# The tail of an attention and quantized feed-forward kernel: last scores and exponentials by tile, small scales moved to GpSimd, decodes moved to ScalarE

## What is computed

```
q     = x + embed[stage][:, None]          # one bias per row
prob  = softmax(q @ f.T)                   # 256x256
a     = prob @ f
xh    = a @ H                              # Hadamard 256x256, scaled
scale = max(max|xh| over the row, 1e-5) / 7
xq    = clip(round(xh / scale), -8, 7) * scale
wq    = ternary(weight) * mean|weight row|
out   = x + xq @ wq.T
```

## Time and profile before

| | |
|---|---|
| median of 3 runs | 108.36 us (107.94 to 108.78) |
| the profiled execution | 108.61 us, span 106.8 us |
| TensorE busy | 97.4 us (91% of the span), 799 products |
| VectorE busy | 87.7 us (82%) |
| ScalarE busy | 76.1 us (71%) |
| GpSimd busy | 47.1 us (44%) |
| DMA | 14.71 MB, mean 138 GB/s |

### The profile page before, as it was taken

How to read it: one execution, slowest core, us unless ns; L and a number is a source line. 1 busy time by engine, 2 the same in 40 slices (tenths; PEclk the granted TensorE clock), 3 DMA queues, 4 the chain that set the end, 5 groups by cost and what they waited for, 6 DMA issues and landing times.

```text
span 106.8 us, 2584 instructions
## 1 busy us (share of the span) xinstructions
PE 97.4 (91%) x799; PEld 90.9 (85%) x799; DVE 87.7 (82%) x216; ACT 76.1 (71%) x200; POOL 47.1 (44%) x66
## 2 busy tenths in 40 slices
PE   5969899999999999999999999999999998995640
PEld 2439799899999999999999999999999998995410
DVE  1085699798989898989989898989898989699880
ACT  3255986969696978787878787878788865780610
POOL 5034699404343435343435353535353534058050
PEclk9999999999999999999999999999999999999855
DMA  3984632425253664947282728282722222202214
GB/s 68 256 298 120 257 112 30 169 53 199 49 173 134 175 215 119 228 111 237 96 227 86 245 68 262 54 289 49 292 51 98 49 98 49 98 0 98 98 53 143
DMA packets 14850, 14.71 MB, mean 138 GB/s; under 512 B 8054, under 2 KB 8956, under 8 KB 14844
## 3 DMA queue, kind: packets, MB, share of 16 engines
q1 hardware_dynamic: 14688, 14.62, 45.1%
q10 hardware_dynamic: 156, 0.01, 0.1%
HBM read 8.73 MB, written 4.19 MB: 121 GB/s over the span
## 4 chain that ended last, share of the span: by engine, by line
PE 72%; DVE 14%; ACT 4%; DMA 3%; issue 3%; ACTq 1%; DVEq 0%
PE score_bank L461 19%; PE xh_bank L461 18%; PE fh_bank L461 12%; PE prob_bank L450 6%; PE out_bank L516 5%; PE f_bank L450 5%; PE q_bank L450 5%; DMA stage_of<-itok_dram 3%; ACT prob L672 2%; DVE prob_lo L841 1%; DVE least_scale L863 1%; DVE fh_lo L841 1%; DVE raw_scale L819 1%; DVE xh_bank L996 1%; DVE result L1002 1%
## 5 line engine op out<-in xcount | busy, mean ns | idle before, releaser
L359 POOL TENSOR_TENSOR result<-scaled,x_all 128x512 f32<-128x512 f32 x13 | 16.7, 1281 | 24.3 <-DVE scaled L827 24.3
L351 POOL TENSOR_TENSOR code<-code,magic 128x512 bf16<-128x512 f32 x13 | 13.5, 1040 | 14.8 <-ACT code L650 14.8
L650 ACT ACTIVATE code<-xh_bank,inv_scale 128x256 f32<-128x256 f32 x30 | 12.8, 486 | 4.8 <-DVE inv_scale L953 2.8
L672 ACT ACTIVATE prob<-score_bank,neg_max 128x256 f32<-128x256 f32 x32 | 15.0, 478 | 0.9 <-DVE neg_max L868 0.9
L841 DVE TENSOR_TENSOR prob_lo<-prob_bank,prob_hi 128x512 fp32r<-128x512 f32 x16 | 11.1, 691 | 5.2 <-ACT prob_hi L662 5.2
L666 ACT CAST fh_hi<-fh_bank 128x512 fp32r<-128x512 f32 x16 | 9.4, 589 | 7.9 <-PE fh_bank L461 7.7
L461 PE MATMUL score_bank<-f_hi,q_hi 128*128 128x256 f32 x64 | 14.1, 302 | 0.3 <-ACT prob L672 0.3
L461 PE MATMUL fh_bank<-had,f_hi 128*128 128x256 f32 x64 | 14.0, 299 | 0.0
L641 ACT CAST f_hi<-f_bank 128x512 fp32r<-128x512 f32 x15 | 8.8, 587 | 5.7 <-PE f_bank L450 5.7
L461 PE MATMUL score_bank<-f_lo,q_hi 128*128 128x256 f32 x64 | 12.8, 282 | 0.0
L461 PE MATMUL score_bank<-f_hi,q_lo 128*128 128x256 f32 x64 | 12.8, 282 | 0.0
(11 more groups left out here) (129 smaller groups left out, 232.5 us busy)
## 6 DMA issues: line engine op xcount, KB each, us to landing
f_nat<-f_dram SPq DMA_DIRECT2D x16, 256.0 KB, 2.8
x_all<-x_dram SPq DMA_DIRECT2D x16, 256.0 KB, 3.0
out_dram<-result SPq DMA_DIRECT2D x14, 256.0 KB, 2.0
out_dram<-result SPq DMA_DIRECT2D x4, 128.0 KB, 1.8
w_raw<-weight_dram SPq DMA_DIRECT2D x1, 256.0 KB, 4.8
code_t<-code SPq DMA_TRANSPOSE x13, 2.5
had_block<-hadamard_dram SPq DMA_DIRECT2D x1, 64.0 KB, 3.9
embed_sb<-embed_dram ACTq DMA_DIRECT2D x1, 6.0 KB
```

Source lines behind the costliest of these rows:

```text
L351: nc.gpsimd.tensor_tensor(as_rows(code16[:, b.k]), as_rows(code), magic[:, :].broadcast_to([P, W]), ALU.subtract).then_inc(code16_ready, 1)
L359: nc.gpsimd.tensor_tensor(result[:, b.k], as_rows(scaled[:, b.k]), x_all[:, b.at], ALU.add).then_inc(result_ready, 1)
L650: return nc.scalar.activation(to[:, t], xh[:, t], ACT.Copy, bias=MAGIC, scale=inv_scale[:, b.k, t:t + 1])
L672: a = nc.scalar.activation(prob[:, t], score_bank[:, t], ACT.Exp, bias=neg_max[:, b.k, t:t + 1], accum_out=row_sum[:, b.k, t:t + 1])
```

## The change

After the loop, five things change. TensorE turns batch 14's probabilities ahead of the last scores; the last scores go into f_bank and q_bank, a tile each with a signal of its own, and VectorE's maximum and ScalarE's exponential follow by tile. On TensorE, mix of 14 stands ahead of 13's ternary products, and the Hadamard products of 15 ahead of the code turn of 13. The two least_scale multiplies and the output scales of 14 and 15 are made on GpSimd; VectorE keeps the reciprocals of the sums, and takes those of batch 14's scales in one instruction. Both decodes of 128x512 are on ScalarE. The last batch's result has its own buffer, last_result, so the wait for batch 13's store is gone. In GpSimd's list a final step (batch 12's result) is drawn behind the two least_scale multiplies.

```diff
@@ tiles and banks
+        last_result = sb("last_result", [P, W], F32)
+        last_score_banks = [f_bank, q_bank]
@@ SyncE, last stores
-                sp.dma_start(out_dram[last.at, :, cols], result[:, last.k, cols]
+                sp.dma_start(out_dram[last.at, :, cols], last_result[:, cols]
@@ GpSimd, after the loop
-            for i in range(B - 2, B + LAG_OUT - 3):
+            for i in range(B - 2, B):
                 step(peeled(i), dma_turns=i - LAG_QUANT < turned_by_dma)
+            for b in (second_last, last):
+                pool.wait_ge(prob_ready, b.at + 1)
+                pool.wait_ge(raw_scale_ready, b.at - 1)
+                nc.gpsimd.tensor_scalar(least_scale[:, b.k], row_sum[:, b.k], MIN_ABS / POS, None,
+                                        ALU.mult).then_inc(least_ready, 1)
+            step(peeled(B), dma_turns=False)
+            pool.wait_ge(last_raw_ready, T)
+            pool.wait_ge(sums_ready, second_last.at + 1)
+            pool.wait_ge(scaled_ready, second_last.at - 1)
+            nc.gpsimd.tensor_tensor(out_scale[:, second_last.k], raw_scale[:, :],
+                                    inv_sum[:, second_last.k], ALU.mult).then_inc(out_scale_ready, 1)
...
+            pool.wait_ge(last_raw_ready, 2 * T)
+            pool.wait_ge(sums_ready, last.at + 1)
+            nc.gpsimd.tensor_tensor(last_out_scale[:, :], last_raw_scale[:, :], inv_sum[:, last.k],
+                                    ALU.mult).then_inc(last_out_scale_ready, 1)
@@ TensorE, after the loop
-            score(last)
             turn_prob(second_last)
+            pe.wait_ge(f_lo_ready, B)
+            pe.wait_ge(q_lo_ready, B)
+            pe.wait_ge(prob_ready, last.at)
+            for t in range(T):
+                product(last_score_banks[t], score_parts(last), [t]).then_inc(score_in_bank, 1)
             times_ternary(fourth_last)
+            times_hadamard(last)
             turn_code(third_last)
-            times_hadamard(last)
             turn_prob(last)
+            mix(second_last)
+            pe.wait_ge(prob_ready, B)
             pe.wait_ge(code_t_ready, third_last.at + 1 - turned_by_dma)
             for t in range(T):
                 mm = ternary_tile(third_last_out_bank, t, third_last)
             mm.then_inc(third_last_out_in_bank, 1)
-            mix(second_last)
@@ ScalarE, after the loop
+            def decode(b):
+                act.wait_ge(code_in_bank, b.at + 1 - turned_by_dma)
+                nc.scalar.activation(code_t[:, b.k].rearrange("p t c s -> p c t s"),
+                                     code_bank[:, 0:C].rearrange("p c (t s) -> p c t s", t=T),
+                                     ACT.Copy, bias=-CODE_ONE * CODE_STEP, scale=CODE_STEP
+                                     ).then_inc(code_t_ready, 1)
+            split_prob(second_last)
             quantize(third_last)
-            split_prob(second_last)
-            exponentials(last)
+            for t in range(T):
+                act.wait_ge(neg_max_ready, last.at + t + 1)
+                a = nc.scalar.activation(prob[:, t], last_score_banks[t][:, t], ACT.Exp,
+                                         bias=neg_max[:, last.k, t:t + 1],
+                                         accum_out=row_sum[:, last.k, t:t + 1])
+            a.then_inc(prob_ready, 1)
             split_fh(last)
             split_prob(last)
+            decode(third_last)
...
                 quantize_tile(last_code, last_xh_banks[t], t, last).then_inc(last_code_ready, 1)
+                if t == 0:
+                    decode(second_last)
@@ VectorE, after the loop
             scales(third_last, out_on_pool=False)
-            maximum(last)
+            inverse_sums(second_last)
+            for t in range(T):
+                dve.wait_ge(score_in_bank, last.at + t + 1)
+                nc.vector.tensor_reduce(neg_max[:, last.k, t:t + 1], last_score_banks[t][:, t],
+                                        AX.X, ALU.max,
+                                        negate=True).then_inc(neg_max_ready, 1)
             split_prob(second_last)
-            decode(third_last)
             scale_out(fourth_last)
+            inverse_sums(last)
             split_fh(last)
             split_prob(last)
-            sums(second_last)
-            sums(last)
...
-            dve.wait_ge(least_ready, B)
+            dve.wait_ge(least_ready, second_last.at + 1)
...
-            for t in range(T):
-                dve.wait_ge(last_raw_ready, t + 1)
-                v = row_inverse(t, second_last, raw_scale)
-            v.then_inc(inv_scale_ready, 1)
+            dve.wait_ge(last_raw_ready, T)
+            nc.vector.reciprocal(inv_scale[:, second_last.k], raw_scale[:, :]).then_inc(inv_scale_ready, 1)
+            dve.wait_ge(least_ready, B)
...
-            decode(second_last)
-            dve.wait_ge(sums_ready, B)
-            for t in range(T):
-                v = row_out_scale(t, second_last, raw_scale, out_scale[:, second_last.k])
-            v.then_inc(out_scale_ready, 1)
-            for t in range(T):
-                row_out_scale(t, last, last_raw_scale, last_out_scale).then_inc(last_out_scale_ready, 1)
...
-            dve.wait_ge(last_out_scale_ready, T)
-            dve.wait_ge(stored[last.k], 16 * last.half)
+            dve.wait_ge(last_out_scale_ready, 1)
...
-                nc.vector.tensor_tensor(result[:, last.k, cols], last_scaled_bank[:, t],
+                nc.vector.tensor_tensor(last_result[:, cols], last_scaled_bank[:, t],
```

More of the change, by code:

```diff
@@ L396, in _ @@
                     step(looped(half, odd))
-            for i in range(B - 2, B + LAG_OUT - 3):
+            for i in range(B - 2, B):
                 step(peeled(i), dma_turns=i - LAG_QUANT < turned_by_dma)
-            third_last, second_last = Batch(0, B - 3), Batch(0, B - 2)
+            third_last, second_last, last = (Batch(0, B - n) for n in (3, 2, 1))
+            for b in (second_last, last):
[9 more added lines that the diff above has]
+                                    inv_sum[:, second_last.k], ALU.mult).then_inc(out_scale_ready, 1)
             pool.wait_ge(third_last_scaled, 1)
@@ L484, in score @@
                 wait(pe, prob_ready, b.at)
-                product(score_bank, [(q_hi[:, b.k], f_hi[:, b.k]), (q_hi[:, b.k], f_lo[:, b.k]),
-                                     (q_lo[:, b.k], f_hi[:, b.k])]).then_inc(score_in_bank, 1)
+                product(score_bank, score_parts(b)).then_inc(score_in_bank, 1)
             def low_half_words(of):
```

17 lines of the change are left out of this document (6 added, 11 removed).

## The result

The changed kernel's median was 106.93 us (106.68 to 107.70, 4 runs) against 108.22 of before in the same comparison; the ratio is 0.9886, with a 95% interval of 0.9845 to 0.9926. A second measurement on another occasion gave 106.92 us (6 runs) and 0.9887 (0.9838 to 0.9936). So it is faster by 1.1%, and 106.8 had been forecast. The profiled execution took 106.84 us with a span of 105.0, where 107.0 and 105.2 were worked out. All medians and ratios here are of executions in the faster of the chip's two states.

What follows compares the result with a forecast made beforehand. The tail was bound by packed TensorE, then VectorE's chain with a held multiply, then a fixed string to the stores. Batch 14's 1.39 plus the clock's 0.23 gave 1.62 us less: profiled 107.0, median 106.8, range 106.1 to 107.8.

Steps and rivals of the forecast that it cites:

- The held multiply: VectorE's 128x2 least_scale multiply before batch 14's maximum, held off by GpSimd's column product; moving it saves 0.87 us.
- The mix: Batch 14's mix on TensorE ahead of batch 13's ternary products: 0.36 for these plus a closed 0.12 hole, 0.48 us earlier.
- One reciprocal for two: VectorE's reciprocals of batch 14's scales in one instruction: 0.28 becomes about 0.16, saving 0.12 us.
- The decode on ScalarE: 128x512 decodes taken as 0.59 us (bounds 0.33 and 0.76); batch 13's hidden in idle time, batch 14's on the path.
- The clock: TensorE stays at full clock for batch 14's ternary products because its standstill is shorter; 0.23 us gained.
- SyncE's queue sets the end: Four final stores issue in order and move by 1.62 us; last at 102.48, later than VectorE's last addition at 102.25.
- Output scales on GpSimd: Last batch's output scales ready at 100.0, wanted by VectorE at 100.36: cover 0.3 us, lag beyond it counts fully.
- Own buffer: Separate buffer for the last result spares VectorE a wait of about 1 us for batch 13's store.
- 1, small waits adding up: Thin covers on GpSimd or ScalarE break in the tail, losing 0.3 to 0.5 us: 107.05 to 107.3; chance 0.20.
- 2, GpSimd holding off the last row scales: GpSimd's large operations block VectorE's 128x1 scale operations of the last tiles: 107.6 us; chance 0.10.
- 3, nothing comes of it: Stall moves to another VectorE instruction, or batch 15's probabilities come late: 108.0 to 108.6 us; chance 0.05.
- 4, colliding stores: Batch 13's store, issued about 1.1 us ahead of the final stores, slows their landing: 109.2 us; chance 0.05.

Runs made afterwards that it cites:

- the run with filling products: Kernel before plus seven unused 128x512 products of zeros on TensorE ahead of the wait for batch 14's codes; median 108.18 us, ratio 0.9990.
- the run with the two forms: Kernel before with each of the tail's 128x2 least_scale multiplies on VectorE written as two of 128x1; median 107.46 us, ratio 0.9914.

## Why the prediction was right

The time, the sign and the mechanism held, and the chain after is the one that was written down. That the sum came out so close in the tail (1.62 forecast, 1.73 measured) is in part luck: the mix was sized 0.25 too low and the reciprocal 0.14 too high. By its steps:

- *The held multiply* was sized 0.87 and measured 0.86 alone, in the kernel that moves nothing else. This was the largest term, and the right one.
- *The mix* was undersized: 0.48 forecast, 0.73 measured. The prediction let turns and products "only" exchange places in a packed queue, and took the hole's width for the price of the wait in it. What a group takes until the next can start depends on what follows and on whether it had to wait. Before had these rows between those of 90.05 and 93.42 in the earlier trace rows:

```profile
91.56 0.60 PE L450 MATMUL prob_bank<-ident,prob 128*128 128x128 f32 x4
92.00 0.60 PE L516 MATMUL out_bank<-tern_t,code_t 128*128 128x256 bf16 x4
92.44 0.39 PE L450 MATMUL code_bank<-ident,code 128*128 128x128 bf16 x4
```

  Batch 12's ternary products took 0.44 ahead of the code turn (92.00 to 92.44) and take 0.36 ahead of the Hadamard products (91.83 to 92.19): 0.08. The turn of the last probabilities took 0.49, after a wait and ahead of ternary products, and takes 0.36 without a wait and ahead of the mix: 0.13. The first instruction after batch 14's exponentials, now a turn and not the scores, starts 0.05 after their end instead of 0.14: 0.09. The other pieces take back 0.05, so that 0.25 is what was missing. Of the last scores the prediction said that the part "costs and saves nothing else"; put back, it costs 0.30 in the tail, of which the sum had the hole's 0.12.
- *One reciprocal for two* was sized 0.12 and saved nothing. From the start of the maximum over 14 to the start of the code turn it is 2.27 in before and 2.29 after. The pair in before overlapped with the second row scale (98.24 against its end at 98.33), while the single one must wait for both. No run put the pair back by itself.
- *The decode on ScalarE* took 0.60 (0.59 taken). From code turn to ternary products 0.99 became 1.09; the sum had given it 0.08 more. That batch 13's would be hidden was right; that the same decode on VectorE would have cost 0.46 in this order was not seen, in the prediction or in the run's expectation. The Trainium skill's rule cited there (page "ScalarE: Activation LUTs", section "Rules for kernel authors") compares the two engines' speed per element. The traces agree that VectorE is the faster one (0.41 for the decode there against 0.60), and it did not decide: what decided was which engine was idle when.
- *The clock* was worth 0.22 (from ternary products to scaling 0.75 became 0.53), sized 0.23, and the run with filling products confirms what it hung on.
- *SyncE's queue sets the end*, forecast, and confirmed by moving two stores out of it.
- *Output scales on GpSimd*: in time, as forecast (99.67, wanted at 100.21). No run put them back by themselves, so what this move is worth stays open; on VectorE there is room for them now, as it waits 0.98 for TensorE ahead of 99.42.
- *Own buffer*: the wait it spares measured 1.38 against about 1, as the sum had taken the wait at the addition, which writes the buffer, while it stands ahead of the scaling before it. At the end it was worth 1.07, with SyncE's queue taking up the rest.

The rivals: 1, small waits adding up, did not come, but only the timelines say so. The tail gained 1.73, not 1.1 to 1.3. By the medians the gain is 1.29 in the first comparison and 1.43 in the second (108.35 to 106.92), so the times alone fit this rival about as well as the forecast. 2, GpSimd holding off the last row scales, falls by the rows: 0.21 each beside GpSimd's large operations, and the run with the two forms had 128x1 multiplies run just as freely. 3, nothing comes of it, is out. 4, colliding stores, is out: the last stores landed in 1.8 to 1.9 us.

## What to carry to other kernels

Look for the instruction that is far longer than its own median: one row with 1251 ns against 150 was half of this change, and giving it another form (two of 128x1) was worth as much as giving it to another engine. When a tail's order is changed, edits hold one another up: undoing the order of the mix alone took back all of the gain and undoing the buffer most of it, moving batch 13's decode back as well as 14's took a quarter, and moving 14's alone took nothing. At the very end look at the queue that issues the last stores; issuing two of four from an idle engine brought about 0.9 us beyond the whole change.

## What was not expected of the hardware

A turn of four 128x128 float32 products takes 0.36 us until the next product can start when TensorE comes from other work and float32 products follow, and 0.44 when the bf16 ternary products follow (91.56 to 92.00 in before). After a wait it is 0.41 to 0.42 and 0.49. So a wait on TensorE costs 0.05 to 0.06 us more than its own length here, and a ternary product behind a turn costs 0.08.

A store's issue took 0.43 to 0.44 us on SyncE for the last result and 0.35 from ScalarE, for the same 128 KB. This is not the engine: in the run without the buffer, where the same two stores come with a pause ahead of each, SyncE issues them in 0.33. In the rows the long issues are those that start 0.04 us after the end of another.

And with the last stores on ScalarE the time outside of the span fell by 0.2 us, in every run of both kernels that have them there.
